# Selective-scan layer with FFN, eight rows of 1024 tokens: the first chunk's order of work, one convolution block on TensorE, and B's first load and first drive in two parts

## The reference

```python
xz = einsum('bld,ed->ble', x, W_in);  xi, z = split(xz, 2)      # 512 channels each
xc = sum(xpad[:, k:k + L, :] * conv_w[:, k] for k in range(4))  # causal conv over 4 tokens
u  = silu(xc + conv_b)
dbl = einsum('blc,ec->ble', u, W_xproj)                         # 16 for dt, 16 for B, 16 for C
dt = softplus(einsum('blr,cr->blc', dbl[..., :16], W_dt) + b_dt)
# per token: 512 channels x 16 states
h  = h * exp(dt[:, :, None] * A) + (dt * u)[:, :, None] * B[:, None, :]
y  = einsum('bcs,bs->bc', h, C)
y  = (y + u * D_skip) * silu(z)
x1 = layernorm(x + einsum('blc,dc->bld', y, W_out))
out = layernorm(x1 + W_down @ (silu(W_gate @ x1) * (W_up @ x1)))  # 768 hidden, int weights / 127
```

## Time and profile before

| | |
|---|---|
| median of 3 runs | 1844.32 us (1843.4 to 1846.78) |
| the profiled execution | 1845.17 us, of which 1843.2 us is the span from the first to the last instruction |
| share of the span busy | PE 95%, ACT 92%, DVE 91%, POOL 81% |
| mean granted clock of TensorE | 0.988 of full |
| first scan of chunk 0 | 57.64 us |
| first scan of chunk 1 | 148.28 us |
| first scan of chunk 2, of chunk 3 | 259.44 us, 369.34 us |

### The profile page before, as it was taken

How to read it: one execution, slowest core, us unless ns; L and a number is a source line. 1 busy time by engine, 2 the same in 40 slices (tenths; PEclk the granted TensorE clock), 3 DMA queues, 4 the chain that set the end, 5 groups by cost and what they waited for, 6 DMA issues and landing times.

```text
span 1843.2 us, 40373 instructions
## 1 busy us (share of the span) xinstructions
PE 1752.4 (95%) x15674; PEld 1213.6 (66%) x15674; DVE 1675.2 (91%) x1946; ACT 1697.6 (92%) x2927; POOL 1494.4 (81%) x847
## 2 busy tenths in 40 slices
PE   6679999999999999999999999999999999999997
PEld 2446676766667676676766667676676766667676
DVE  4999999999989999899989999999998999989984
ACT  5899999999999999999999999999999999999981
POOL 1997997879888787987879788787997879798950
PEclk9899999999999999999999999999999999999999
DMA  7030121301313120131301213130131311112000
GB/s 205 2 98 21 4 115 15 115 14 4 125 4 115 15 93 35 3 116 15 115 15 26 102 3 116 15 115 13 4 115 15 115 15 54 74 4 104 24 2 23
DMA packets 171342, 100.56 MB, mean 55 GB/s; under 512 B 139392, under 2 KB 157568, under 8 KB 162960
## 3 DMA queue, kind: packets, MB, share of 16 engines
q1 hardware_dynamic: 171152, 97.98, 18.3%
HBM read 88.52 MB, written 9.44 MB: 53 GB/s over the span
## 4 chain that ended last, share of the span: by engine, by line
PE 52%; ACT 25%; DVE 10%; issue 9%; POOL 3%; ACTq 0%; POOLq 0%; DVEq 0%
PE ring L1132 21%; PE tp L1111 15%; PE yb L1125 8%; ACT hT L684 7%; ACT decay L677 7%; DVE h L882 6%; PE ring L1220 4%; POOL drive L549 2%; ACT xi L695 1%; ACT sz L700 1%; ACT res L743 1%; ACT acc L693 1%; ACT u L710 1%; DVE acc L903 1%; ACT sz L714 1%
## 5 line engine op out<-in xcount | busy, mean ns | idle before, releaser
L549 POOL TENSOR_TENSOR drive<-dtu,b_all 128x1024 f32<-128x1024 f32 x512 | 1212.5, 2397 | 45.4 <-DVE h L882 41.2
L677 ACT ACTIVATE decay<-dt,a_neg 128x512 f32<-128x512 f32 x1024 | 702.7, 711 | 25.8 <-DVE h L882 24.7
L1111 PEld LDWEIGHTS tp<-ident,h 128*128 128x128 f32 x4096 | 462.0, 141 | 273.6 <-issue 153.1
L1111 PE MATMUL tp<-ident,h 128*128 128x128 f32 x4096 | 578.4, 278 | 64.8 <-ACT hT L684 47.9
L684 ACT ACTIVATE hT<-tp 128x512 f32<-128x512 f32 x1024 | 591.4, 606 | 46.8 <-PE tp L1111 44.9
L882 DVE TENSOR_TENSOR_SCAN h<-decay,h,drive 128x512 f32<-128x512 f32 x512 | 622.5, 1270 | 11.8 <-ACT decay L677 11.6
L882 DVE TENSOR_TENSOR_SCAN h<-decay,drive 128x512 f32<-128x512 f32 x512 | 592.9, 1210 | 23.1 <-ACT decay L677 21.3
L1125 PE MATMUL yb<-hT,diag_c 128*32 128x128 f32 x8192 | 273.9, 276 | 0.0
L1125 PEld LDWEIGHTS yb<-hT,diag_c 128*32 128x32 f32 x8192 | 209.9, 110 | 67.5 <-issue 44.4
L1132 PE MATMUL ring<-xt,w_in 128*128 128x512 f32 x512 | 238.3, 600 | 6.4 <-ACT xi L695 3.8
L903 DVE SCALAR_TENSOR_TENSOR acc<-xi,cw,acc 128x512 f32<-128x512 f32 x192 | 155.6, 830 | 29.4 <-ACT xi L695 25.4
(11 more groups left out here) (128 smaller groups left out, 1612.2 us busy)
## 6 DMA issues: line engine op xcount, KB each, us to landing
b_all<-bc_scratch SPq DMA_DIRECT2D x64, 1024.0 KB, 9.2
xt<-in_xT SPq DMA_DIRECT2D x16, 512.0 KB, 4.7
res<-in_x SPq DMA_DIRECT2D x16, 512.0 KB, 10.7
out<-res SPq DMA_DIRECT2D x15, 512.0 KB, 2.9
c_col<-bc_scratch SPq DMA_DIRECT2D x256, 2.0 KB, 2.5
bc_scratch<-dbl SPq DMA_DIRECT2D x16, 64.0 KB, 1.6
w_g<-in_w_gT SPq DMA_DIRECT2D x1, 768.0 KB, 7.1
w_u<-in_w_uT SPq DMA_DIRECT2D x1, 768.0 KB, 7.5
```

The source lines that it names most:

```text
L549: tt(drive[:, j % 4, :, :], src, b_all[:, n:n + 2, :], ALU.mult).then_inc(g_dr, 1)
L677: act(decay[decay_slot(k.parity, i)][:, :], dt[:, cb, :], ACT.Exp, scale=a_neg[:, cb, n:n + 1]).then_inc(a_da, 1)
L1111: last = nc.tensor.transpose(tp[g % 2][:, b * P:(b + 1) * P], h[:, h_slot(k.parity, q), t0:t0 + TS, :].rearrange("p t s -> p (t s)"), iden ...
```

## The change

Five things, all in the run-up and in chunk 0. The tables of chunks 1 to 15 stay.

1. The four `_FIRST` tables are new. On DVE only the clamp of the second dt half stands ahead of the first scan; the convs of chunk 1 stand behind scans 12 and 18. On ACT the work for chunk 1 is spread over quads 1 to 4, with all silus behind the decay of (4, 3). On POOL `dtu` of blocks 2 and 3 stands behind unit 9, and `heads` behind unit 10.
2. In the run-up, the conv of block 3 is four matmuls on TensorE with diagonal weights (`first_taps`: ident times a tap, made by POOL in the last `h` slot) into the third decay bank. ACT then has only the copy of `xi` there, and takes silu straight from the bank. It takes the place of two filler matmuls.
3. The product `xproj` of chunk 0 waits for `u` block by block, not for all four.
4. B's first load is two loads of two rows (semaphores f_b and l_b[0]), and the first drive unit is two instructions of one row each; scan 0 waits for the first alone.
5. In the run-up the table load for exp and log stands behind the copy of `dbl`, not ahead of it.

```diff
 DVE_FIRST = {
-    (0, -1): [("clamp", 1), ("conv", 0, 0), ("conv", 0, 1), ("conv", 1, 0), ("max", 1), ("conv", 1, 1), ("conv", 2, 0), ("conv", 2, 1)],
-    (7, 3): [("conv", 3, 0), ("conv", 3, 1), ("skip", 0)], (13, 2): [("skip", 1), ("clamp", 0)],
...
+    (0, -1): [("clamp", 1)], (0, 3): [("max", 1)], (3, 0): [("conv", 0, 0)],
+    (4, 2): [("conv", 0, 1), ("conv", 1, 0), ("conv", 1, 1), ("conv", 2, 0), ("conv", 2, 1), ("conv", 3, 0), ("conv", 3, 1)],
...
+        def first_taps(tap):
+
+            return h[:, HS - 1, tap * TS:(tap + 1) * TS, :].rearrange("p t s -> p (t s)")
...
                     if with_b:
-                        load_b(g)
+                        if g == 0:
+                            src = bc_dram[0:2, :].rearrange("(o n) t -> o n t", o=1)
+                            eng.dma_start(b_all[:, 0:2, :], src.to_broadcast([P, 2, T])).then_inc(f_b, 16)
+                            src = bc_dram[2:4, :].rearrange("(o n) t -> o n t", o=1)
+                            eng.dma_start(b_all[:, 2:4, :], src.to_broadcast([P, 2, T])).then_inc(l_b[0], 16)
+                        else:
+                            load_b(g)
...
+                if first and j == 0:
+                    eng.wait_ge(f_b, 16)
+                    eng.wait_ge(f_dtu, 1)
+                    tt(drive[:, 0, 0, :], dtu[:, 0, :], b_all[:, 0, :], ALU.mult).then_inc(f_dr, 1)
+                    tt(drive[:, 0, 1, :], dtu[:, 0, :], b_all[:, 1, :], ALU.mult).then_inc(g_dr, 1)
+                    return
...
-            for cb in range(CB):
+            for cb in range(CB - 1):
                 silu_u(k0, cb)
+            eng.wait_ge(f_conv, 1)
+            act(u[:, 0, CB - 1, :], decay[DECAYS - 1][:, :], ACT.Silu, bias=cbias[:, CB - 1:CB]).then_inc(a_u, 1)
+            copy_dbl(k0)
             nc.scalar.preload_act_table_set(EXP_LN_SET)
-            copy_dbl(k0)
...
                 if what == "xproj":
-                    for _ in range(2):
-                        mm(tp[0][:, :], hT[:, 0, 0:P], hT[:, 0, :], start=True, stop=True)
+                    eng.wait_ge(f_diag, KW)
+                    eng.wait_ge(a_xi, 2 * CB)
+                    for tap in range(KW):
+                        last = mm(decay[DECAYS - 1][:, :], first_taps(tap), xi[:, CB - 1, tap:tap + T],
+                                  start=tap == 0, stop=tap == KW - 1)
+                    last.then_inc(f_conv, 1)
                     eng.wait_ge(l_w, ALL_LOADED)
                 room(at)
-                dense(Chunk(0, 0), what, i)
+                if what == "xproj":
+                    for cb in range(CB):
+                        eng.wait_ge(a_u, cb + 1)
+                        x_proj_block(Chunk(0, 0), cb)
+                else:
+                    dense(Chunk(0, 0), what, i)
```

More of the change, by code:

```diff
@@ L98 @@
 PE_FIRST = {
[L99 to L103, removed]
@@ L130 @@
+    (4, 2): [("conv", 0, 1), ("conv", 1, 0), ("conv", 1, 1), ("conv", 2, 0), ("conv", 2, 1), ("conv", 3, 0), ("conv", 3, 1)],
+    (11, 0): [("clamp", 0)], (12, 1): [("skip", 0)], (12, 3): [("skip", 1)], (13, 2): [("max", 0)],
+    (14, 3): [("skip", 2)],
 }
 POOL_FIRST = {
-    (0, -1): [("dtu", 1)], (2, 1): [("first_diag", 0)], (3, 0): [("first_diag", 1), ("first_diag", 2)],
-    (5, 0): [("first_diag", 3)], (8, 1): [("heads", 0)], (15, 0): [("gate", 0)],
-    (15, 1): [("gate", 1), ("dtu", 0), ("gate", 2), ("diag", 0)],
+    (2, 0): [("first_diag", 0)], (3, 0): [("first_diag", 1), ("first_diag", 2)],
@@ L135 @@
+    (4, 1): [("dtu", 1), ("first_diag", 3)], (5, 0): [("heads", 0)], (13, 0): [("gate", 0)],
+    (15, 0): [("dtu", 0)], (15, 1): [("diag", 0), ("gate", 1), ("gate", 2)],
 }
@@ L538, in drive_unit @@
                 wait(eng, v_h, k.count(STEPS, 2 * (j - 4) + 2))
-                if cb == 0 and n % 4 == 0:
+                if first and j == 0:
[4 more added lines that the diff above has]
+                    return
+                if cb == 0 and (n == 2 if first and n < 4 else n % 4 == 0):
                     wait(eng, l_b[n // 4], k.count(16, 16))
@@ L543, in drive_unit @@
                     tt(dtu[:, 1, :], dt[:, 1, :], u[:, 0, 1, :], ALU.mult).then_inc(f_dtu, 1)
-                if first and j in (0, 8):
-                    eng.wait_ge(f_dtu, j // 8 + 1)
+                if first and j == 8:
+                    eng.wait_ge(f_dtu, 2)
                 elif j % 16 == 0:
@@ L807, in _ @@
             eng.wait_ge(l_cv, 16 * len(conv_loads))
-            for cb in range(CB):
+            for cb in range(CB - 1):
                 copy_xi(k0, cb)
-            for cb in range(CB):
+            eng.wait_ge(p_xi, CB)
+            act(xi[:, CB - 1, KW - 1:], bank(k0, "xi", CB - 1)[:, :], ACT.Copy).then_inc(a_xi, 2)
+            for cb in range(CB - 1):
                 silu_u(k0, cb)
+            eng.wait_ge(f_conv, 1)
+            act(u[:, 0, CB - 1, :], decay[DECAYS - 1][:, :], ACT.Silu, bias=cbias[:, CB - 1:CB]).then_inc(a_u, 1)
+            copy_dbl(k0)
             nc.scalar.preload_act_table_set(EXP_LN_SET)
-            copy_dbl(k0)
             eng.wait_ge(l_w, ALL_LOADED)
@@ L1165, in in_z, with x_proj_block @@
                                               for d in range(DH)], p_z)
+            def x_proj_block(k, c):
+                for b in range(2):
+                    last = mm(bank(k, "xproj", 0)[b * P // 2:b * P // 2 + R + 2 * N, 0:T // 2], w_x[:, c, :],
+                              u[:, k.parity, c, b * T // 2:(b + 1) * T // 2],
+                              start=c == 0, stop=c == CB - 1)
+                if c == CB - 1:
+                    last.then_inc(p_x, 1)
             def x_proj(k):
@@ L1170, in x_proj @@
                 for c in range(CB):
-                    for b in range(2):
-                        last = mm(bank(k, "xproj", 0)[b * P // 2:b * P // 2 + R + 2 * N, 0:T // 2], w_x[:, c, :],
-                                  u[:, k.parity, c, b * T // 2:(b + 1) * T // 2],
-                                  start=c == 0, stop=c == CB - 1)
-                last.then_inc(p_x, 1)
+                    x_proj_block(k, c)
             def dt_proj(k, cb):
```

28 lines of the change are left out of this document (21 added, 7 removed), and 32 rows, old and new, of the table ACT_FIRST.

## The result

The median went from 1845.55 us (4 runs, 1843.4 to 1847.16) to **1833.68 us** (4 runs, 1832.94 to 1834.07): ratio 0.9934, 95% interval 0.9923 to 0.9946, or 11.9 us less. The forecast was 1827.3 with 1820 to 1836 around it: the direction and the range hold, and the gain is about 5 us smaller than the sum said (11.9 instead of 17.0). The same kernel timed again on another chip gave 1832.80 against 1845.67, ratio 0.9933 (0.9920 to 0.9947).

What follows compares the result with a forecast made beforehand. PE bounds chunk 1 onward, nothing is full in chunk 0, so only chunk 1's start can move. Run-up, scans and convs put it at 131.3 instead of 148.28: 1843.2 less 17.0 is 1826.2 of span, median 1827.3, range 1820 to 1836.

Steps and rivals of the forecast that it cites:

- the sum: Whole kernel: chunk 1's first scan at 131.3 instead of 148.28, 17.0 us earlier, so a median of 1827.3 us.
- Run-up: Start to scan 0: dbl's copy at 20.4, first exp 24.0, dtu 26.05, scan 0 at 30.0, 27.6 us earlier.
- rival 1: Run-up stays slow with PE's clock at 0.50: first scan 5 us later, 1832 us; chance 0.07.
- xproj by blocks: Run-up on PE: three blocks run during block 3's silu, the last takes 0.4 us; dbl's copy at 20.4, 3.7 earlier.
- Scans 0 to 18, "POOL is last": Chunk 0 up to the convs: POOL sets the pace, unit 9 ends at 55.9 and scan 18 at 57 us.
- rival 2: Chunk 0, quads 1 to 4: ACT waits for products at half clock, +5 to +9 us, 1832 to 1836; chance 0.13.
- a sign that the forecast is wrong: Chunk 0: ACT rather than DVE having the long waits between 30 and 57 us would contradict the forecast.
- Eleven convs: DVE behind scan 18: about three convs share 6.6 us with POOL, eight take 6 alone; 11.2 us, ending at 68.2.
- Scans 19 to 63: DVE from the convs to chunk 1: 45 scans without convs take 63.1 us, so chunk 1 starts at 131.3.
- From chunk 1 on: Chunk 1 to the end: same instructions in the same order take the same time, chunk 1 still 111 us long.
- Rival 4: Chunk 0: clock stays at 0.50 and PE becomes the bound; chunk 1 21 us later, 1865 us; chance 0.04.

Runs made afterwards that it cites:

- the second profile: The changed kernel itself, nothing edited, timed and profiled a second time: 1832.80 us.
- the clamp at skip 0: Against the changed kernel, VectorE's clamp of chunk 1's first dt half moved five scans later, directly ahead of skip 0 in chunk 0: 1830.60 us, ratio 0.9923.
- the twelve runs above: The follow-up runs: eleven variants with parts of the change undone or edits added, and the changed kernel repeated; 1830.03 to 1839.97 us.

## Why the prediction was right in its direction and too large in its gain

- **Run-up.** The times look right step by step: dbl 20.29 for 20.4, exp 23.84 for 24.0, dtu 25.89 for 26.05, scan 0 at 30.01 for 30.0; taps and xproj at clock 1.00 (rival 1 out). But this was luck in part: 1.1 us of it came from an early landing of the first loads. With the landing of the kernel before, scan 0 is at 31.23, so the sum for the run-up was 1.2 too short. The step that failed is *xproj by blocks*. The forecast had three of four blocks run beside the last silu and 0.4 us behind it. Here is the second profile, with the first product at 7.58 as in rows 5:

```profile
15.92 3.67 PE L1409 MATMUL decay<-xi,h 128*128 128x512 f32 x8 [0.84 <-ACT xi L837]
19.52 1.94 PE L1201 MATMUL ring<-u,w_x 128*48 128x256 f32 x16
21.50 0.78 ACT L746 ACTIVATE dbl<-ring 48x256 f32<-48x256 f32 x2 [1.18 <-PE ring L1201]
```

  On TensorE xproj stands behind the taps, which end at 19.6. Its sixteen passes take 1.94 at full clock and the silu only 0.69, so the copy of dbl waits 1.18 and comes at 21.50, not 20.4: 0.8 of the 1.1 are this, 0.3 the taps. B's first load took 4.2 us from its issue at 22.72 to the first drive at 26.91, not the 3.1 of the forecast, but that cost only 0.3 behind dtu. By the Trainium skill (ScalarE: Activation LUTs, What ACT_TABLE_LOAD costs) a switch would also have a drain of 1.38 us. Here the load ends at 22.37 and the next activation starts at 22.38.
- **Scans 0 to 18, "POOL is last".** This step failed: convs from 60.9 instead of 57. POOL did nearly keep the forecast's pace (unit 9 ended at 56.7 for 55.9), but it was not last. What came later was ScalarE's decay, behind transposes and products at half clock. That is rival 2's mechanism, which had 0.13, and the prediction had named such waits of ScalarE as a sign that the forecast is wrong. Where the clock stood high at 46 to 50, the same order gave 58.95, 29.0 behind scan 0 where the forecast had 27.
- **Eleven convs.** The mechanism was right, its size was for the wrong moment: 9.54 instead of 11.2, because DVE came late and two of the three POOL instructions were over. Started at 58.95 they take 10.95.
- **Scans 19 to 63.** The mis-sized term: 67.05 (70.37 to 137.42) instead of 63.1. I took the stretch of the kernel before with its two clamps at their lengths there, 1.48 and 2.35. In the new order the first of them falls into POOL's run of fifteen drives and takes 4.97, 3.5 more; that is most of the 3.9. The last one, 2.38, is as long as before. With the clamp at skip 0 the stretch is 61.5.
- **The sum.** Chunk 1 was forecast 17.0 us earlier and came 10.9: 3.9 lost ahead of the convs, 1.7 won in them, 3.9 lost behind (of which the place of the clamp is 3.2). With that place mended it is 16.9. That this is the forecast's 17.0 is luck: other terms are off and cancel.
- **From chunk 1 on.** Right but for 1.6 us each way: chunk 1 got shorter (I had said 111), and the end of the kernel longer. Rival 4 is out, with a mean clock of 0.89 in chunk 0. Busy times by stretch near the end, first before, then after:

```profile
1804.00:1808.00 4.00, 3.92 (x11) 3.28 (x12) 1.39 (x7) 0.45 (x2) 0.70 (x1) 0.61 0.00 0
```

```profile
1792.00:1796.00 4.00, 3.91 (x9) 3.19 (x10) 1.12 (x5) 0.13 (x2) 0.70 (x1) 0.50 0.00 0
1796.00:1800.00 4.00, 4.00 (x17) 3.35 (x17) 0.69 (x1) 0.50 (x1) 0.00 (x0) 0.83 0.00 0
```

  From the last chunk's first scan to the end it is 154.3 us in the one profile of before (1688.9 to 1843.2), 155.9 in the changed kernel's, and 154.6 to 155.9 in the twelve runs above. The rows lie 32 to 40 us before the end: the clock is low for a while in both kernels there, and lower after the change. Whether that profile of before was a lucky one or the end has got slower stays open.

## What to carry to other kernels

Where GpSimd holds up a VectorE instruction, put that instruction where GpSimd has to wait for VectorE anyway. Here that was worth 3.2 us, while another form of the instruction or a place two scans later left it waiting as long as before. A stretch copied from the profile before with "the same instructions" keeps its length only if the neighbours of each of them stay the same too. On an engine that works in order, a block that waits for its own input also waits for everything that stands ahead of it. And before an edit is credited with a few microseconds of one trace, look at a second trace of the unedited kernel: here the landing of the first loads alone moved 1.1 us, and a spell of half clock went with up to 1.9.
